# A convolution kernel's opening reordered: weights, first fills and first products spread over other engines

## What is computed

```python
def _L0_conv_ref(x, coupler_w, coupler_b, weight, bias):
    logits = conv1x1(x, coupler_w) + coupler_b          # 8 sets
    sel = softmax(logits, axis=1); sel = sel / sel.sum(axis=1, keepdims=True)
    conv = conv3x3(x, weight).reshape(b, s, oc, h, w) + bias
    return einsum('bschw,bshw->bchw', conv, sel)
x = x + _L0_conv_ref(_gn(x), ...)
```

## Time and profile before

| | us |
|---|---|
| median of 3 runs | 336.83 (336.24 to 336.9) |
| profiled execution, device time | 337.13 |
| its span in the trace | 335.3 |
| PE busy | 323.8 |
| DVE busy | 277.4 |
| POOL busy | 229.6 |
| ACT busy | 110.8 |

### The profile page before, as it was taken

How to read it: one execution, slowest core, us unless ns; L and a number is a source line. 1 busy time by engine, 2 the same in 40 slices (tenths; PEclk the granted TensorE clock), 3 DMA queues, 4 the chain that set the end, 5 groups by cost and what they waited for, 6 DMA issues and landing times.

```text
span 335.3 us, 5416 instructions
## 1 busy us (share of the span) xinstructions
PE 323.8 (97%) x1684; PEld 153.7 (46%) x1684; DVE 277.4 (83%) x499; ACT 110.8 (33%) x167; POOL 229.6 (68%) x329
## 2 busy tenths in 40 slices
PE   8995999999999999999999999999999999999994
PEld 8533344444544444444544444444544444444441
DVE  2799799997799988887799878887799877777786
ACT  1688162175221162175221162175221111111112
POOL 3700696899994698899854788899864788334343
PEclk9999899999999999999999999999999999999999
DMA  6799389009960397019870496009820496010002
GB/s 201 312 264 220 76 209 223 23 2 233 224 192 0 89 239 179 3 33 241 201 173 3 125 227 152 0 30 239 178 57 0 120 236 152 0 42 28 3 1 70
DMA packets 30374, 41.93 MB, mean 125 GB/s; under 512 B 2128, under 2 KB 23248, under 8 KB 29968
## 3 DMA queue, kind: packets, MB, share of 16 engines
q1 hardware_dynamic: 29184, 37.78, 46.7%
q10 hardware_dynamic: 1168, 3.89, 3.9%
HBM read 12.56 MB, written 4.72 MB: 52 GB/s over the span
## 4 chain that ended last, share of the span: by engine, by line
PE 87%; DMA 4%; DVE 3%; POOL 2%; SPq 1%; issue 1%; ACT 1%; DVEq 0%; ACTq 0%
PE pair L397 54%; PE pair L409 18%; PE pair L405 14%; DMA op<-v_tail 2%; DMA x_raw<-x 2%; POOL v_pts L1091 2%; PE side L387 1%; DVE last_mixed L853 1%; DVE v_pts L975 0%; SPq L305 0%; ACT w_head L632 0%; DVE pair L828 0%; DVE half L837 0%; DVE v_tail L987 0%; DVE high L829 0%
## 5 line engine op out<-in xcount | busy, mean ns | idle before, releaser
L397 PE MATMUL pair<-w_head,op 128*128 128x512 f16 x864 | 234.8, 381 | 3.9 <-DMA op<-v_tail 3.8
L397 PEld LDWEIGHTS pair<-w_head,op 128*128 128x128 f16 x864 | 84.1, 98 | 106.0 <-DMA op<-v_tail 4.4
L409 PE MATMUL pair<-w_tail,op 128*128 128x512 f16 x288 | 109.5, 380 | 0.0
L590 ACT ACTIVATE m_sb<-pair 128x512 f32<-128x512 f32 x72 | 42.9, 596 | 196.7 <-PE pair L409 189.2
L1114 POOL TENSOR_TENSOR quarter<-half 128x256 f32<-128x256 f32 x71 | 52.7, 742 | 61.7 <-DVE half L837 60.9
L828 DVE TENSOR_TENSOR pair<-pair,sel_now 128x512 f32<-128x512 f32 x71 | 49.4, 696 | 35.1 <-PE pair L409 34.5
L837 DVE TENSOR_TENSOR half<-pair,high 128x512 f32<-128x512 f32 x71 | 49.1, 692 | 10.2 <-DVE high L829 1.0
L405 PE MATMUL pair<-w_tail,op_two 128*128 128x512 f16 x144 | 55.0, 382 | 0.0
L812 DVE TENSOR_TENSOR pair<-pair,m_sb 128x512 f32<-128x512 f32 x72 | 49.6, 689 | 0.0
L814 DVE TENSOR_TENSOR pair<-m_sb,pair 128x512 f32<-128x512 f32 x72 | 49.3, 684 | 0.0
L829 DVE TENSOR_TENSOR high<-pair,sel_now 128x512 f32<-128x512 f32 x71 | 48.3, 680 | 0.0
(11 more groups left out here) (109 smaller groups left out, 198.8 us busy)
## 6 DMA issues: line engine op xcount, KB each, us to landing
op<-v_head SPq DMA_DIRECT2D x14, 600.0 KB, 8.1
x_res<-x_pix SPq DMA_DIRECT2D x8, 576.0 KB, 6.5
op_two<-v_head SPq DMA_DIRECT2D x14, 300.0 KB, 9.0
op<-v_tail SPq DMA_DIRECT2D x14, 300.0 KB, 6.5
op<-v_head SPq DMA_DIRECT2D x14, 288.0 KB, 8.4
out<-y_out SPq DMA_DIRECT2D x7, 576.0 KB, 4.0
x_raw<-x ACTq DMA_DIRECT2D x3, 1152.0 KB, 10.5
w_raw<-weight SPq DMA_DIRECT2D x3, 768.0 KB, 8.7
```

Of the source, the lines that this page charges most:

```text
L397: nc.tensor.matmul(dst, op[b][:, 0, j, at + r * PW:at + r * PW + P], w_head[:, j, r, :], start=fresh and r == 0, stop=False, skip_group_ch ...
L409: return nc.tensor.matmul(dst, op[b][:, 1, j, at:at + P], w_tail[:, j, 0, :], start=False, stop=True, skip_group_check=True)
L590: act.activation(m1_sb[:, i % LOOK, :], pair[i % SETS_OF_BANKS][:, 0, :], ACT.Copy).then_inc(m1_copied, 1)
```

## The change

It touches the opening, the first four tiles of round 0 and one step of the later rounds' preparation. What it does:

- The four constants (matrices, coupler weights, coupler bias, bias) are laid side by side by the host and come in one load on SP; four small loads on ACT's queue go.
- POOL does `inverse_deviation(0)` after two thirds of its differences instead of after the first op of the last third.
- ACT does the head of point 1 before any `bound_of`. DVE does point 0's head before the tails of point 1.
- The first fills of points 0 and 1 are split by point, each with its own semaphore; those of points 2 and 3 come in `first_fill_late`. `load_res(0, 0)` goes behind the rest fills of points 0 and 1 and `load_ahead(1)` behind the last kernel tail.
- The third kernel row's points are made by POOL (`row_two`) in SBUF, not by PE and DVE. The rest of the heads of points 1 and 0 go from ACT to POOL (`rest_head`), the coupler's heads from DVE to ACT.
- DVE's and ACT's lists are put in another order; DVE writes the soon selection's weights in one step (`weights_soon`) and the sums after tile 0's products. The softmax for the other tiles goes one tile later.
- In tiles 0 to 3 of round 0 the even pixel's products are made by ACT (`even_products`), the odd one's by DVE (`multiply_odd`).
- `combine` goes from DVE at tile 4 to ACT at tile 6; ACT's sums and squares go one tile later.
- `warm_small` is cut from 28 to 18, with three more after `group_sums`, and `WARM_WIDE` from 6 to 4.

The names SOON, LOOK and `SEEDED = 0` mean: the first six tiles' selection is made ahead, seeds run two tiles ahead, and no tile's seed is left to another engine. The diff, cut to its core:

```diff
-WARM_SMALL = 28
-WARM_WIDE = 6
+WARM_SMALL = 18
+WARM_MORE = 3
+WARM_WIDE = 4
...
-BIAS_FIRST_AT = (0, 0, 3, 4, 10, 13)
+BIAS_FIRST_AT = (0, 0, 4, 5, 10, 13)
...
-SUMS_AT = (3, 3)
-SQUARES_AT = (4, 5)
+SUMS_AT = (4, 4)
+SQUARES_AT = (5, 6)
+EVEN_TILES = 4
+SEEDED = 0
...
+        consts = sb("consts", [P, 3 * P + 2 * SETS + SETS + C])
+        mean_mat, diff_mat, eye_mat = (consts[:, k * P:(k + 1) * P] for k in range(3))
+        cw_pair = consts[:, 3 * P:3 * P + 2 * SETS]
...
+        row_sums = y_out[1][:, :, :, :].rearrange("p t a c -> p (t a c)")
+        w_outer = row_sums[:, 0:N]
+        w_pt1 = [pair[2][:, 0, :], pair[2][:, 1, :], row_sums[:, N:2 * N]]
...
+            def first_fill_head(k):
+
+                cols, below = slice(0, PW + FIRST_PAIRS), slice(0, FIRST_PAIRS)
+                wait(h_first, 2 - k)
+                sp.dma_start(op[0][0:C, 0, k, cols], v_head[0:C, k, cols]).then_inc(first_pt[k], 16)
+                sp.dma_start(op[0][C:P, 1, k, below], v_head[0:C, k, PW:PW + FIRST_PAIRS]).then_inc(first_pt[k], 16)
+
+            def first_fill_tail(k):
+
+                cols = slice(0, PW + FIRST_PAIRS)
+                wait(t_first, k + 1)
+                sp.dma_start(op[0][C:P, 0, k, cols], v_tail[0:C, k, cols]).then_inc(first_pt[k], 16)
+
+            def first_fill_late():
+
+                pts, cols, below = slice(2, NP), slice(0, PW + FIRST_PAIRS), slice(0, FIRST_PAIRS)
+                heads = v_head[0:C, pts, :]
+                wait(h_first, NP)
+                sp.dma_start(op[0][0:C, 0, pts, cols], heads[:, :, cols]).then_inc(first_late, 16)
+                sp.dma_start(op[0][0:C, 1, pts, cols], heads[:, :, cols]).then_inc(first_late, 16)
+                sp.dma_start(op[0][C:P, 1, pts, below], heads[:, :, PW:PW + FIRST_PAIRS]).then_inc(first_late, 16)
+                sp.dma_start(op_two[0][0:C, :, cols], heads[:, :, cols]).then_inc(first_late, 16)
+                wait(t_first, NP)
+                sp.dma_start(op[0][C:P, 0, pts, cols], v_tail[0:C, pts, cols]).then_inc(first_late, 16)
...
-            first_fill(0, 0)
+            for k in range(2):
+                first_fill_head(k)
+                first_fill_tail(k)
+            first_fill_late()
+            rest_fill(0)
             load_res(0, 0)
-            first_fill(1, 0)
-            first_fill(0, 1)
-            first_fill(1, 1)
+            rest_fill(1)
...
+            warm_small(WARM_MORE)
+            for r in range(2):
+                pe.wait_ge(w_loaded[r], 16)
+                kernel_point1(r, (0, 2, 1)).then_inc(w_point1, 1)
...
-            kernel_point1(2, (2, 1)).then_inc(w_point1, 1)
...
-            pe.wait_ge(first_in[0], 16 * (F_PARTS + 1))
+            pe.wait_ge(first_pt[0], 16 * F_PARTS)
             for i in range(3):
                 first_point(i, 0, 0, i == 0)
-            for i in range(3):
-                first_point(i, 1, 0, i == 0)
+            pe.wait_ge(first_pt[1], 16 * (F_PARTS + 1))
+            for i in range(SEEDED, 3):
+                first_point(i, 1, 0, i == SEEDED)
...
+            def combine(m):
+
+                act.wait_ge(group_done, m)
+                act.wait_ge(centered, m * 3)
...
+            def even_products(i):
+
+                act.wait_ge(sel_copied, 1)
+                act.wait_ge(half_done, i + SETS_OF_BANKS)
+                act.wait_ge(y_done, 2 * i + 1)
+                for k in range(SETS):
+                    y = pair[i % SETS_OF_BANKS][:, 0, k * C:(k + 1) * C]
+                    last = act.activation(y if k < SETS // 2 else high[:, 0, k - SETS // 2, :], y, ACT.Copy,
+                                          scale=sel_w[:, 2 * i, k:k + 1])
+                last.then_inc(even_done, 1)
...
+                    if n == 0 and 0 <= i - LOOK < EVEN_TILES:
+                        even_products(i - LOOK)
                     if i >= copied:
                         copy_m1(i, n)
+                    if n == 0 and i == 4:
+                        exponentials(0, 1)
...
+                    if more and i == SQUARES_AT[1]:
+                        combine(n + 1)
...
+            def coupler_heads():
+
+                act.activation(cw_pts[:, 0, 1:3, :], cw_pair.unsqueeze(1).to_broadcast([P, 2, 2 * SETS]), ACT.Copy,
+                               scale=half_scale[:, 1:2]).then_inc(c_heads, 1)
+                act.activation(cw_pts[:, 0, 0, :], cw_pair, ACT.Copy, scale=minus_half_scale[:, 1:2]).then_inc(c_heads, 1)
...
-            act.dma_start(bias_all[:, :], bias.partition_broadcast(P)).then_inc(small_loaded, 16)
-            act.dma_start(cb_all[:, :], coupler_b.partition_broadcast(P)).then_inc(small_loaded, 16)
-            act.wait_ge(cleared, 1)
-            for b in range(2):
-                act.dma_start(cw_pair[C * b:C * b + C, b, :], coupler_w).then_inc(small_loaded, 16)
...
+            def fill_beside(k):
+
+                cols = slice(0, PW + FIRST_PAIRS)
+                act.wait_ge(h_first, 2 - k)
+                act.dma_start(op[0][0:C, 1, k, cols], v_head[0:C, k, cols]).then_inc(first_pt[k], 16)
+                if k == 1:
+                    act.dma_start(op_two[0][C:P, :, cols],
+                                  v_head[0:C, 1, cols].unsqueeze(1).to_broadcast([C, 2, PW + FIRST_PAIRS])).then_inc(first_pt[1], 16)
+
+            first_heads(1, 0)
             bound_of(0)
-            first_heads(1, 0)
+            fill_beside(0)
             bound_of(1)
+            fill_beside(1)
             bound_of(2)
-            fill_beside()
-            act.wait_ge(scale_ready, 1)
             for k in range(2, NP):
                 edge(0, k)
             first_heads(2, 0)
             act.wait_ge(w_chain, W_STEPS)
             for r in range(K):
                 w_heads_of(0, slice(r, r + 1))
-            load_ahead(1)
             first_heads(3, 0)
+            coupler_heads()
             w_heads_of(1)
-            first_heads(1, 1)
-            first_heads(0, 1)
             act.wait_ge(w_mix_loaded, 16)
             act.activation(w_mix_head[:, :, :], w_mix[:, :, :], ACT.Copy, scale=scale[:, 0:1]).then_inc(w_mix_heads, 1)
+            copy_m1(0, 0)
             w_heads_of(2)
-            copy_m1(0, 0)
+            copy_m1(1, 0)
             w_heads_of(3)
             act.wait_ge(w_tails, 6)
             act.activation(w_tail[C:P, 3, 1, :], w_tail[C:P, 2, 1, :], ACT.Copy, scale=-1.0).then_inc(w_minus, 1)
-            copy_m1(1, 0)
+            load_ahead(1)
             first_heads(2, 1)
...
+            def weights_soon():
+
+                px = slice(0, SOON_PIX)
+                dve.wait_ge(prep, 14)
+                dve.scalar_tensor_tensor(sel_w[:, px, :], logit[:, px, :], undo[:, 0:1], spread(top[:, px], SETS),
+                                         ALU.mult, ALU.mult).then_inc(sel_copied, 1)
...
+            def multiply_odd(i):
+                dve.wait_ge(y_done, 2 * i + 2)
+                dve.tensor_tensor(y[:, 0:SETS // 2, :], y[:, 0:SETS // 2, :], weights[:, 0:SETS // 2, :], ALU.mult) \
+                    .then_inc(low_done, 1)
+                dve.tensor_tensor(high[:, 1, :, :], y[:, SETS // 2:SETS, :], weights[:, SETS // 2:SETS, :], ALU.mult) \
                     .then_inc(high_done, 1)
...
+                    if begin and i < EVEN_TILES:
+                        multiply_odd(i)
+                        if i == 0:
+                            divide_again(0, 0)
+                        dve.wait_ge(even_done, i + 1)
+                        halve(i, n)
+                    elif i + 1 < TILES or more:
                         multiply(i, n)
...
             first_input_point(0)
-            input_tails_of(1, 0, 1)
             first_head()
             input_tails_of(0, 0, 2)
+            input_tails_of(1, 0, 2)
             first_input_point(1)
+            kernel_point2(0)
             weight_bound()
-            kernel_point2(0)
+            kernel_point2(1)
             scales()
-            kernel_point2(1)
+            input_tails_of(2, 0, 3)
             first_point_tail(0)
             first_point_tail(1)
-            kernel_point2(2)
             first_point_tail(2)
-            input_tails_of(2, 0, 3)
             input_tails_of(3, 0, 4)
+            coupler_tails()
+            input_tails_of(1, 1, 1)
             second_point_tails()
-            coupler_parts()
-            input_tails_of(1, 1, 1)
             input_tails_of(0, 1, 2)
+            seed(0, 0)
             mixed_tails()
             last_row_tail(2)
-            seed(0, 0)
+            last_row_tail(3)
             with_bias(0, 0)
             maximum(0, 0)
             less_maximum(0, 0)
-            last_row_tail(3)
+            seed(1, 0)
             add_up(0, 0)
             invert(0, 0)
             divide(0, 0)
-            seed(1, 0, (0,))
             add_up_again(0, 0)
-            seed(1, 0, (1,))
             invert_again(0, 0)
-            divide_again(0, 0)
-            selection(0, sel_now_parts, sel_copied, 0)
+            weights_soon()
```

(27 more changed lines are left out.)

204 lines of the change are left out of this document (106 added, 98 removed).

## The result

The changed kernel takes **338.75 us** (median of 7 runs, 337.66 to 339.94) against 336.71 for the kernel before on the same chip: 1.0062 times as long, 95% interval 1.0045 to 1.0079. I had forecast 334.7, with 336.9 as the upper end and a chance of 0.17 for slower. The profiled execution took 337.98 us, span 336.2, so the trace shows 0.85 of the 2.0 us lost; the rest lies in executions of which there is no trace. How far the runs spread, the experiments come back to.

The account below looks back on a forecast made before the run. Time could be won only ahead of 37 us, where late tails, slow clock and VectorE's list held TensorE. Terms -0.1, +0.58, -2.58, +1.2 and -1.21 sum to -2.1: 336.83 to 334.7 us, range 332.9 to 336.9.

Parts of the forecast that it names:

- the yardstick: Judge the change by how far 39.56 us moves, when TensorE takes up tile 3's first points, and which later waits grow.
- Part 7: After TensorE's restart: waits of 0.3 and 0.4 us for halves of tiles 3 and 4, `combine` no effect; sum nothing.
- some 1.0 us in two: Kernel before, after 39.56 us: TensorE's waits for `half`, taken as some 1.0 us in two waits.
- the signs I gave for being wrong: Scale after 20; VectorE tails over 1.6 us; clock 0.5 after the wait; TensorE waiting for tile 3's half over 1 us, or `group_sums`.
- Part 1: Opening statistics and x heads: `rstd` 0.64 us sooner, and x landing 0.1 us sooner with the small loads merged.
- Part 2: Opening, weights' bound: `weight_bound` starts at 17.70 instead of 17.12, +0.58 us; scale set at 19.31.
- Part 4: VectorE's serial list from `scale` to the selection, 17.0 us: steps taken out or moved save 2.58 us.
- Part 5: GpSimd running beside VectorE in the opening: three VectorE tails slowed by 0.4 us each, +1.2 us, selection at 34.9.
- Part 3: First fills cut by point: tails land near 28 to 29 instead of 33.2; 3.3 us of waiting and the slow clock go.
- Part 6: Selection to TensorE's restart: 2.62 us with even products on ScalarE; restart at 37.5, -2.0; TensorE idles some 2.6 us.
- Rival (a): TensorE's clock goes slow in the 2.6 us wait, costing 1.7 us; about 336.3; chance 0.20.
- Rival (c): ScalarE's queue in round 0: x loaded late holds its sums and what follows; 337.8 at 3 us late; chance 0.07 with (e).

Follow-up runs that it names:

- e5: Kernel before the change, with only GpSimd's two bias steps moved from tiles 3 and 4 to tiles 4 and 5: 338.68 us, 1.0048 times the kernel before.
- e16: Kernel with bias steps back, scales on ScalarE and waits filled (334.65 us), its bias steps and their softmax again one tile later: 337.28 us.
- e17: Kernel before the change, with ScalarE's four small loads issued only once x has landed: 336.32 us, 0.9982 times the kernel before.
- e7: e4 with unused matmuls filling TensorE's opening waits, seven ahead of the first products and eight in the first point's wait: 336.00 us.
- e9: e4 with GpSimd waiting for the weights' scales between the first and second step of the third kernel row: 337.31 us.
- e6: e4 with nine unused matmuls in TensorE's wait for half of tile 0: 335.95 us.
- e4: Changed kernel with GpSimd's bias steps and the softmax of the other heads put back to tiles 3 and 4: 336.14 us.

## Why the prediction was wrong

- **The step that failed is the yardstick with Part 7**: "by how much does 39.56 move" was carried to the end one for one, with "nothing" for what follows. The waits of 0.3 and 0.4 us that Part 7 forecast for TensorE came in size (0.29 at 54.73, 0.37 at 59.58), but for the halves of tiles 4 and 5, not 3 and 4. I set them against "some 1.0 us in two" of the kernel before, and that was a misreading: the earlier trace rows counts waits of weight loads (PEld), which run beside the products; TensorE itself was busy for 47.05 of the 47.2 us from 36.8 to 84. Above all I weighed the halves against TensorE only. GpSimd's `finish` waits for the same halves, and its list to the logits had no slack: the way from the restart to the logits took 46.12 us instead of 43.74. The `BIAS_FIRST_AT` line stood in the diff and was never priced; it costs 1.9 us alone (e5), and 2.6 together with its softmax on the improved opening (e16). None of my rivals named GpSimd behind 37 us; of the signs I gave for being wrong only one came, a VectorE tail over 1.6 us (1.70 at 22.32), and it belongs to the opening. TensorE did not wait over 1 us for half of tile 3.
- **The opening was right in sum and wrong in its terms.** Restart 38.02 against 37.5 forecast. x landed 2.3 us sooner, not 0.1 (Part 1, settled by e17); so the weights' bound came at 15.99 instead of 17.70 (Part 2 gave +0.58, it was -1.13). Most of that was given back: from the bound to the scales took 2.8 instead of 1.61 us, since two scale steps were held. Part 4's list gave some 1.9 us instead of 2.58: from the scales to the selection it took 16.66, of which Part 5's price is 1.56. No run takes that difference apart. The slow clock of Part 3 moved instead of going, to the first products (0.68 from 16 to 26 us); filling that wait (e7) left the restart where it was.
- **Part 5, GpSimd beside VectorE**: the three tails cost 0.57, 0.89 and about 0.1 more instead of three times 0.4, in sum 1.6 against 1.2. The mechanism was right; I missed the smallest steps. The Trainium skill, "SBUF — State Buffer", section "Who interferes with whom", also lists `tensor_scalar` among the operations that, when their operands allow it, can take the pair of ports shared with GpSimd, and has whoever comes second blocked fully. I used only its clause on two inputs; the 128x2 steps (0.15 alone, up to 0.93 beside GpSimd) agree with the other one.
- **Part 6** held: the restart came 2.56 us after the selection's end (35.46); 2.62 was forecast, and TensorE's wait of 2.38 for some 2.6. The selection was 0.56 later than forecast.
- **Rival (a)** occurs in some executions and not in others: 1.24 us in e7's. (Its own terms add up to 336.1, not 336.3.) Rival (c), with x landing late behind ScalarE's queue, did not occur: the sums ran at 44.88, against 44.9 forecast.
- With the bias steps back, the scales on ScalarE and the waits filled, the kernel takes 334.65 us. That this equals my 334.7 is luck: it has edits that the forecast didn't know, and the terms of the forecast were off both ways.

## What to carry to other kernels

A step that comes sooner wins only as much as every list behind it comes sooner too, and a step that comes later costs nothing only where its list has slack. Measure that slack from the end of each engine's last product to its reader, not by the busy share, and take off the hop that also lies there when the reader stands waiting (0.15 us here). Price every line of a diff on every engine, the constants that place steps in tiles too. An idle engine that can hold up a busy one is not free to be filled: a step moved onto it can hold steps a tenth as long as itself.

## What the hardware showed unexpectedly

- Four 128x2 VectorE steps took 0.43 us in all (e9) or 3.24 (e6), by whether GpSimd ran beside them; the reciprocal between them (0.17) and the step that reads PSUM (0.16) were not held in any of these traces.
- Four small loads, together 0.04 MB in 448 packets, held up 1.15 MB of x by 2.5 us. The Trainium skill, "DMA: Bandwidth & Descriptors", section "Why small descriptors are slow (HBM only)", gives a fixed cost for each packet as the reason why small ones are slow; the runs show the delay, not its cause.
- After the same wait of 2.38 us the clock was 1.00 in some executions (the changed kernel, e4) and 0.50 from 38 to 40 us in another (e7).
